# Edge sums of a graph network: one semaphore increment per four matmuls, and Vector operands moved to PSUM

## The reference, cut to what matters

```
# layer 0 (attention with 8 heads)
msg = feat[src] * a[:, :, None]                      # a: one weight per edge and head
out = segment_sum(msg, dst, num_segments=N)
# layer 1 (edge features, mean over the heads)
agg = segment_sum(wbar[:, None] * msg, dst, n)       # msg needs node_feats[src] + edge_feats
deg = segment_sum(ones, dst, n)
# layer 3 (attention again, plus an edge from each node to itself)
out = segment_sum(h[src] * alpha[:, :, None], dst, num_segments=n)
```

## Time and profile before

| | us |
|---|---|
| median of 3 runs | 6046.71 (6040.01 to 6052.1) |
| the profiled execution, its own time | 6077.0 |
| its span | 6075.2 |
| `gat_sum`, first to last matmul of the sum | 607.3 to 950.9 |
| `edge_sum`, the same | 1859.3 to 2200.2 |
| `loops_sum`, the same | 5399.0 to 5732.8 |
| POOL busy over the whole span | 1827.1 (30%) |
| mean granted TensorE clock of the profiled execution | 0.822 |

### The profile page before, as it was taken

One profiled execution on the slowest core, in us unless ns is written; L12 is line 12 of the kernel. 1 busy time (PEld: TensorE's weight loads), 2 busy tenths in 40 slices (PEclk: granted clock), 3 DMA queues, 4 the chain that ended last, 5 costly groups with the idle time before them and its releaser, 6 DMA issues. The chain is left out here.

```text
span 6075.2 us, 67322 instructions
## 1 busy us (share of the span) xinstructions
PE 4117.0 (68%) x18035; PEld 2874.2 (47%) x18037; DVE 2746.0 (45%) x6601; ACT 906.2 (15%) x1972; POOL 1827.1 (30%) x1518
## 2 busy tenths in 40 slices
PE   0691874556805676766898999989945826646539
PEld 0450543334404454533566766767635813334337
DVE  4674655225657665587102011020151256475558
ACT  0200001111000012137102021020212310000012
POOL 2475770126645830100000000000002056657400
PEclk9895986556957887898998999989957968878759
DMA  3364983224627920013542433414222225724300
GB/s 114 89 213 125 312 278 104 73 71 139 216 77 247 293 90 16 4 63 162 178 130 65 140 106 95 131 62 141 74 72 74 64 58 163 217 88 145 97 27 21
DMA packets 476271, 734.24 MB, mean 121 GB/s; under 512 B 67999, under 2 KB 349148, under 8 KB 471575
## 3 DMA queue, kind: packets, MB, share of 16 engines
q1 hardware_dynamic: 339515, 504.54, 25.8%
q0 software_dynamic: 81376, 175.99, 10.4%
q10 hardware_dynamic: 55154, 51.01, 2.5%
HBM read 594.23 MB, written 136.80 MB: 120 GB/s over the span
## 5 line engine op out<-in xcount | busy, mean ns | idle before, releaser
L744 PE MATMUL gin_up_sums<-gin_ring,gin_acc 125*128 125x250 f32 (+1 forms) x4000 | 1069.6, 427 | 23.2 <-ACTq L777 23.2
L744 PEld LDWEIGHTS gin_up_sums<-gin_ring,gin_acc 125*128 125x128 f32 x4000 | 755.8, 189 | 331.4 <-ACTq L777 24.2
L726 DVE BATCH_NORM_STATS2 gin_up_stat<-gin_mlp_z x160 | 77.8, 487 | 1160.5 <-ACT gin_mlp_z L774 1160.5
L2295 POOL IOTA two_seats_pid<- 125x1 f32 x1 | 0.1, 138 | 1617.6 <-ACTq L2292 1617.6
L2892 PE MATMUL edge_sum_part<-edge_ring_rows,edge_sum_hot 128*125 x832 | 237.4, 446 | 116.0 <-DVE edge_sum_hot L1692 61.2
L3020 POOL DMA_INDIRECT edge_ring_rows<-edge_table,src_e x203 | 256.9, 1266 | 166.8 <-PE edge_sum_part L2892 110.4
L2892 PE MATMUL loops_sum_part<-loops_ring_rows,loops_sum_hot 128*125 x832 | 239.0, 450 | 99.3 <-issue 54.8
L3250 PE MATMUL adj_counts_part<-adj_counts_far,adj_counts_low 128*128 128x325 bf16 x1032 | 207.0, 334 | 105.3 <-DVE adj_counts_far L3231 40.5
L3020 POOL DMA_INDIRECT gat_ring_rows<-gat_table,src_e x203 | 243.2, 1198 | 98.0 <-issue 59.2
L3020 POOL DMA_INDIRECT loops_ring_rows<-loops_table,src_e x203 | 237.0, 1168 | 105.4 <-issue 56.1
L2892 PEld LDWEIGHTS edge_sum_part<-edge_ring_rows,edge_sum_hot 128*125 128x125 f32 x832 | 178.5, 221 | 174.7 <-issue 142.0
(11 more groups left out here) (804 smaller groups left out, 7702.7 us busy)
## 6 DMA issues: line engine op xcount, KB each, us to landing
gin_ring<-gin_adj SPq DMA_DIRECT2D x100, 937.5 KB, 4.8
gin_ring<-gin_adj SPq DMA_DIRECT2D x100, 625.0 KB, 3.9
edge_sum_own<-edge_attr_in SPq DMA_DIRECT2D x97, 512.0 KB
gin_adj<-adj_counts_tile SPq DMA_DIRECT2D x25, 1562.5 KB
gat_sum_ef<-edge_attr_t_in SPq DMA_DIRECT2D x128, 256.0 KB
gat_gat_held<-edge_attr_t_in SPq DMA_DIRECT2D x64, 256.0 KB
pre<-gat_gat_held ACTq DMA_DIRECT2D x124, 128.0 KB
gat_ring_rows<-pre SPq DMA_DIRECT2D x31, 512.0 KB
```

What stands on the lines that cost most here:

```text
L726: v.bn_stats(statf[:, bass.ds(i * 12 + (h * 6 + f * UNITS * 6), 6)], z1f[:, nodes(i, h, f * N)]).then_inc(stats, 1)
L744: mm = pe.matmul(sums[h][k][:, 0:n * P].rearrange("p (t n) -> p t n", n=P), acc[:, t, k * 128:(k + 1) * 128], ring[0:P, q, 0:n, c * P:(c + ...
L2295: pool.iota(pid[:], pattern=[[0, 1]], base=0, channel_multiplier=1, allow_small_or_imprecise_dtypes=True).then_inc(made, 1)
```

## The change

Three things are changed. First, the four matmuls of a quad give one increment of four, on the last of them, in place of one each. Second, the numbers 0 to 124 are copied once per stage into a PSUM bank (`numbers`), and the compares read them there. Third, in `sum_heads` the weights are copied into another PSUM bank (`scales`) in blocks of 512 numbers per partition: a weight row has 8 numbers in `gat_sum` and 16 in `loops_sum`, so a block serves 64 or 32 chunks, and there are 7 or 13 blocks. The copy behind the rows and the multiplication read the weights from that bank. The vector engine waits for its own earlier instructions ahead of each block, and for the block after it.

```diff
+        numbers = st.ps("numbers", [EP, 512])
+        IN_PSUM, scales_in = 512 // WH, st.sem("scales_in")
+        scales = st.ps("scales", [EP, 512])[:].rearrange("p (c w) -> p c w", w=WH)
...
-                    make_hot(v, g, hot, s, j, summed, hot_ready)
-                    n = chunks_in(s, j)
+                    make_hot(v, numbers, g, hot, s, j, summed, hot_ready)
+                    n, c = chunks_in(s, j), s + j
                     if n:
                         k = j % RING
+                        if c % IN_PSUM == 0:
+                            many = min(IN_PSUM, C - c)
+                            if c > 0:
+                                v.wait_ge(msg_ready, 2 * c)
+                            v.tensor_copy(scales[:, 0:many, :], weight[:, c:c + many, :]).then_inc(scales_in, 1)
+                            v.wait_ge(scales_in, c // IN_PSUM + 2)
+                        w = c % IN_PSUM
                         ahead.wait_for_rows(v, loaded, ring, s, j)
-                        v.tensor_copy(rows[:, k:k + n, D:], weight[:, bass.ds(s + j, n), :]).then_inc(msg_ready, n)
+                        v.tensor_copy(rows[:, k:k + n, D:], scales[:, w:w + n, :]).then_inc(msg_ready, n)
                         msg = rows[:, k:k + n, 0:D].rearrange(by_head, h=H)
-                        v.tensor_tensor(msg, msg, weight[:, bass.ds(s + j, n), 0:H].unsqueeze(3).to_broadcast([EP, n, H, HD]), ALU.mult).then_inc(msg_ready, n)
+                        v.tensor_tensor(msg, msg, scales[:, w:w + n, 0:H].unsqueeze(3).to_broadcast([EP, n, H, HD]), ALU.mult).then_inc(msg_ready, n)
...
+                v.tensor_copy(numbers[:, 0:P], g.iota[0:EP, 0:P]).then_inc(scales_in, 1)
+                v.wait_ge(scales_in, 1)
...  (sum_edges: the same two lines with a semaphore of its own, and)
-                        v.tensor_scalar(hot[:, (j + n) % HOTS, :], g.iota[0:EP, 0:P], g.place_s[:, bass.ds(s + (j + n), 1)],
+                        v.tensor_scalar(hot[:, (j + n) % HOTS, :], numbers[:, 0:P], g.place_s[:, bass.ds(s + (j + n), 1)],
...  (make_hot)
-    v.tensor_tensor(hot[:, k:k + QUAD, :], g.iota[0:EP, 0:P].unsqueeze(1).to_broadcast([EP, QUAD, P]),
+    v.tensor_tensor(hot[:, k:k + QUAD, :], numbers[:, 0:P].unsqueeze(1).to_broadcast([EP, QUAD, P]),
...  (multiply_quad)
-        pe.matmul(part[0:P, bass.ds(bank, 1), 0:width].rearrange("p a d -> p (a d)"), hot[:, k, :],
-                  rows[:, bass.ds(slot, 1), 0:width].rearrange("p a d -> p (a d)"), start=False, stop=True, skip_group_check=True).then_inc(summed, 1)
+        mm = pe.matmul(part[0:P, bass.ds(bank, 1), 0:width].rearrange("p a d -> p (a d)"), hot[:, k, :],
+                       rows[:, bass.ds(slot, 1), 0:width].rearrange("p a d -> p (a d)"), start=False, stop=True, skip_group_check=True)
+    mm.then_inc(summed, QUAD)
```

More of the change, by code:

```diff
@@ L99 @@
 assert EARLY_CHUNKS[-1] < CS and RING // QUAD % EIGHT == 0
-assert T <= COUNT_MASK
+assert T <= COUNT_MASK and T + 3 * QUAD < RING and SETS >= QUAD and HOTS % QUAD == 0
 assert CS - LOOPS * RING < TAIL and T + 2 * QUAD < RING and RING % HOTS == 0
@@ L1656, in sum_edges @@
         part = st.ps("part", [128, SETS, 512])
+        numbers, numbered = st.ps("numbers", [EP, 512]), st.sem("numbered")
         hot_ready, mixed, summed, empty, copied = (st.sem(n) for n in ("hot_ready", "mixed", "summed", "empty", "copied"))
@@ L1702, in _ @@
                 v.memset(rows[:, :, D], 1.0).then_inc(empty, 1)
+                v.tensor_copy(numbers[:, 0:P], g.iota[0:EP, 0:P]).then_inc(numbered, 1)
+                v.wait_ge(numbered, 1)
                 v.wait_ge(chunks_in_place, 16)
@@ L2870, in wait_for_rows, with make_hot @@
     eng.wait_ge(rows_in[sem], (s + j // RING * RING) * (16 * QUAD // RING) + (before[sem] + 16 * chunks_in(s, j)))
-def make_hot(v, g, hot, s, j, summed, hot_ready):
+def make_hot(v, numbers, g, hot, s, j, summed, hot_ready):
     k = j % HOTS
     v.wait_ge(summed, s + (j + QUAD))
-    v.tensor_tensor(hot[:, k:k + QUAD, :], g.iota[0:EP, 0:P].unsqueeze(1).to_broadcast([EP, QUAD, P]),
+    v.tensor_tensor(hot[:, k:k + QUAD, :], numbers[:, 0:P].unsqueeze(1).to_broadcast([EP, QUAD, P]),
                     g.place_s[:, bass.ds(s + j, QUAD)].unsqueeze(2).to_broadcast([EP, QUAD, P]), ALU.is_equal).then_inc(hot_ready, QUAD)
```

## The result

The changed kernel took 5942.12 us (median of 4 runs, 5939.26 to 5953.57), the kernel before, beside it, 6043.36 (4 runs). The ratio is 0.985, with the 95% interval [0.9825, 0.9875] (so written from here on), and 101 us lie between the medians. The profiled execution took 5940.6 us of its own, against 6077.0 before.

A forecast was written before the change was run, and what follows sets the result against it. GpSimd's unbroken gathers bound the three stages, held by Vector instructions with two SBUF tensors. Terms -43 - 44 + 3 + 0 + 1 = -83 us; 6046.7 - 82.6 = 5964 us, range 5940 to 6005.

The forecast's parts named there:

- Step 1: In `gat_sum` and `loops_sum`, one operand in PSUM frees the held gathers, whole surplus gone: -43 and -44 us.
- The rival that the hold is by the other input: Vector instruction's other input or output, still in SBUF, holds the gathers; nothing released, 6051 us; chance 0.10.
- What is late next: `loops_sum` follows the gather train, -44 us; `gat_sum`, with three limits within a few us, takes 301 us, -43.
- The rival "POOL waiting for PE in `gat_sum`": `gat_sum` stops at transfers or a lower matrix clock, gaining 20 us, `loops_sum` 42; 5985 us; chance 0.15.
- Step 2: Copies of numbers and weights into PSUM, 0.7 us per weight block, mostly hidden by Vector idle time: +3 us.
- Step 3: Vector multiplication, compare and copy behind the rows cost the same out of PSUM, the copy 226 ns: no change.
- The slower rival: Multiplication L1294 reads repeated numbers from PSUM at half rate, the vector engine becomes the bound; 6117 us; chance 0.05.
- Step 4: In `edge_sum` the addition keeps both tensors in SBUF, so gathers stay held: 0 us, bounds -8 and +6.
- Step 5: One increment per quad saves the matrix engine nothing, 0 us; later waits for free places cost 1 us in all.

The follow-up runs named there:

- the third occasion: Later timing session: the changed kernel again, unaltered, against the kernel before on the same chip, increments late; 1.004 [1.0027, 1.0054], 6107 us.

## Why the prediction was right, and where it was not

**The whole.** 5964 us forecast, 5942 measured; the gain was 101 us and not 83. That the time came out near the forecast was in part luck: the occasion was one without late increments, which the prediction knew nothing of. On the third occasion the same kernel took 6107 us and gained nothing, with the gathers released just the same.

**Step 1, the operands release the gathers: right on every occasion.** Means of 946 and 945 ns against the forecast of 950; the slowest gather 958 ns. The rival that the hold is by the other input is out: the earlier trace rows and the experiment with the addition out of PSUM differ in the second input alone. Of the two statements in the Trainium skill, SBUF — State Buffer, section "Who interferes with whom", the traces bear out the contention of an instruction with two SBUF inputs, and not that generating descriptors escapes it: here a gather takes up to 2.0 us beside such an instruction, and 0.95 beside the same one with one input in PSUM. Two SBUF tensors are not the only thing that holds a gather, however. Of the 64 gathers issued in `gat_logits`, 40 take over 1 us before the change, up to 1.77, and 29 do after it. Here one runs beside a compare (L996) of one bfloat16 tensor, and ends 0.83 us behind it (timeline of the kernel before):

```profile
292.10 1.41 POOL L3027 DMA_INDIRECT gat_ring_rows<-gat_table,src_e  x1 [0.30 <-issue]
292.14 0.54 DVE L996 TENSOR_SCALAR gat_logits_hot<-gat_logits_lows,low_of 125x400 bf16<-125x400 bf16 x2
```

The float32 compare of one tensor in `edge_sum` showed no such hold. The prediction took its free gather from this very stage and did not mention the held ones. No run changed L996, so what makes it hold is open.

**What is late next: right for the first result, wrong as a statement on the kernel.** The step says "So the stage follows the train down". It did, 343.9 to 294.2 and 334.2 to 279.1 us, 7 and 11 us further than the -43 and -44 forecast. On the other occasions the stages stayed at 331 to 359 us with gathers just as free. The step left out the round through `summed`, because it added busy times and took the matrix engine's count as there when the matmul ends. The earlier trace rows held the warning: 52.6 us of idling before the compare. The profile of before was itself one with late increments (53 and 47 of them), while the runs that gave its median, 30 us lower, need not have been. The rival "POOL waiting for PE in `gat_sum`" had the right sign to look for; its cause was taken to be transfers or clock, and its price, 20 us, was far too small: on the third occasion the gain was less than nothing.

**Step 2, copies: right in size.** The block took 684 ns, forecast 0.7 us. What they cost on the path was not measured by itself, and whether they stay covered where increments come late is not shown. **Step 3: right** for both two-tensor operations (1211 and 673 ns, before 1216 and 672) and for the copy (221 ns, forecast 226). The slower rival, repeated numbers at half rate, is out.

Where increments come late, the change costs 0.4%. The vector engine's busy time in the three stages is then 34 us more than in the profile of before, 24 of them in `edge_sum`. Of the parts, numbers alone gave 1.002 and weights alone 1.0015, neither clear of no change; both with one increment per matmul gave 1.0018 beside them and 1.0042 and 1.0035 elsewhere. That this added work is what lengthens the round is argued, not shown.

**Step 4, `edge_sum` 0, bounds -8 and +6: the term that was mis-sized.** The profiles give -8 (341.5 to 333.4); on equal terms, against the kernel with SBUF numbers, it is -12. The step named both effects: the compare did get slower, by 38 ns in duration (forecast up to 60), and the gathers did fall out of step. The second outweighed the first there, 62 gathers over 1 us where there were 89. Where increments come late, the numbers in PSUM shortened nothing: 348.9 us in the changed kernel and 342.4 in the kernel beside it with the numbers in SBUF.

**Step 5, increments 0: holds where it was tested.** One increment per quad alone gave 1.0003 and 0.9996; with the operands in PSUM, 1.004 and 1.0042. PE's records keep their pitch: 16 still take 3.82 us (timeline of PE in `gat_sum`, kernel after), as in the earlier trace rows.

```profile
707.07 3.82 PE L2907 MATMUL gat_sum_part<-gat_ring_rows,gat_sum_hot 128*125 x16 [0.19 <-issue]
```

The estimated 24 us that the rule on the cost per increment would have given (the Trainium skill, TensorE: Matmul & The Clock Gate, section "The cost: per-tile semaphore tail") were not found. All these runs were made with late increments, however. With increments on time every kernel that was profiled had one per quad, so a part of the 101 us could be theirs.

**The account of the 101 us.** The stages give 50 + 8 + 55 = 113, the rest 23, together 136, the difference of the two profiled executions. The profile of before took 34 us more than the median of its runs, and the changed kernel shows a like difference outside the stages between its two occasions: 157.6 us in all, 135.6 in the stages, 22 outside. So I put the 23 down to the occasion, and with them some 11 us of the 113, to make up the 34. That leaves about 102, which is the measured gain by construction and not a check of it. How much of `gat_sum` and `loops_sum` was hold and how much was late count in that profile is not known, since the kernel before was never profiled with its increments on time.

**Open.** Why the increments come late on some occasions. That goes with missing records, so it could be the recording itself or something that disturbs both; no run separates them.

## What to carry to other kernels

If GpSimd issues gathers without rest, look at which Vector instructions run beside them: one with two SBUF tensors holds a gather until it ends, and one of the tensors in PSUM frees it at no cost to the instruction (1211 and 673 ns against 1216 and 672), though a copy has to bring it there. Read the gathers' durations for other holders too, as L996 is here. Before booking such a gain, follow the round that returns the buffers (count, producer, consumer, count) and see how long its waits already are. And compare parts of a change only with the whole run beside them on the same chip at the same time: here four parts measured on one occasion and the whole on another suggested an interplay of the parts, which vanished when the whole was run beside them.

## What the runs showed of the hardware

- A semaphore's increment from the matrix engine can reach the waiting engines many us after the recorded end of the matmul, several at once: 9.0 to 12.5 us for the four of the stretch above. Those from the vector engine stand 0.01 us behind their instruction in the same trace. The same program differs by 165 us (2.8%) between occasions with and without this.
- A gather's issue (0.95 us alone) is held beside a Vector instruction with two SBUF tensors, up to 2.03 us in all in the kernel before, and not beside the same one with one tensor in PSUM (958 ns at most over `gat_sum` and `loops_sum`). It is also held beside a compare of one bfloat16 tensor (1.41 us).
- A compare of one tensor with a scalar (128x125) takes 399 ns out of PSUM and 361 out of SBUF; with two tensors, 673 and 672 ns, the place of one of them makes no difference.
- An addition of 1024 elements per partition takes 1220 ns, of 512 elements 686, of 256 elements 417: an estimated 150 ns of each do not depend on the size.
